# Moving the homes of the rounded weights by 256, 128 and 64 bytes, away from the remainder that their moving tiles have

## What is computed

```python
def mamba(x):                       # H=1024, DIN=2048, N=16, K=4, R=64
    x, z = split(x @ in_proj_w)     # input projection, 1024 -> 4096
    xc = silu(causal_conv(x) + conv_b)
    dt, Bm, Cm = rmsnorm of three slices of (xc @ x_proj_w.T)
    dt = softplus(dt @ dt_proj_w.T + dt_bias)
    y = selective_scan(xc, dt, -exp(A_log), Bm, Cm)
    return ((y + D * xc) * silu(z)) @ out_proj_w.T

def cross_attention(x, ctx):        # 16 heads of 96, 4 key/value heads, 1536 keys
    q, k, v = x @ Wq.T, [ctx, x] @ Wk.T, [ctx, x] @ Wv.T
    return softmax(q @ k.T / sqrt(96)) @ v @ Wo.T

def ffn(x):                         # 1024 -> 3584 -> 1024
    return (silu(x @ w1.T) * (x @ w3.T)) @ w2.T

x = layernorm(x + mamba(x))
x = layernorm(x + cross_attention(x, ctx))
x = layernorm(x + ffn(x))
```

## Time and profile before

| | |
|---|---|
| median of three runs | 3108.57 us |
| lowest and highest | 3108.5 and 3111.01 us |
| span of the profiled execution | 3110.0 us |
| granted TensorE clock, mean over the span | 0.965 of 2.4 GHz |
| TensorE matmul busy | 2874.5 us, 92% |
| VectorE busy | 2392.1 us, 77% |
| GpSimd busy | 1703.0 us, 55% |
| ScalarE busy | 1576.3 us, 51% |
| instructions | 35600, of them 11962 matmul records |

### The profile page before, as it was taken

One profiled execution on the slowest core, in us unless ns is written; L12 is line 12 of the kernel. 1 busy time (PEld: TensorE's weight loads), 2 busy tenths in 40 slices (PEclk: granted clock), 3 DMA queues, 4 the chain that ended last, 5 costly groups with the idle time before them and its releaser, 6 DMA issues. The chain is left out here.

```text
span 3110.0 us, 35600 instructions
## 1 busy us (share of the span) xinstructions
PE 2874.5 (92%) x11962; PEld 2040.6 (66%) x11962; DVE 2392.1 (77%) x2147; ACT 1576.3 (51%) x2679; POOL 1703.0 (55%) x952
## 2 busy tenths in 40 slices
PE   8996688888888988999999999989979999999998
PEld 7872344443222356887888888867758888887886
DVE  6568999999999957334777777765798888875667
ACT  4449555555665543214888888862332333334443
POOL 0004999999999933404887888851025444430034
PEclk9995799999989999999999999999989999999999
DMA  4228876766865662332111111215235555557554
GB/s 149 84 78 271 270 196 168 184 156 159 259 189 146 189 244 95 109 116 69 36 34 35 35 36 36 69 55 183 78 129 190 178 185 186 184 177 262 193 175 147
DMA packets 217400, 445.83 MB, mean 143 GB/s; under 512 B 33677, under 2 KB 47757, under 8 KB 215117
## 3 DMA queue, kind: packets, MB, share of 16 engines
q1 hardware_dynamic: 179502, 390.73, 40.5%
q10 hardware_dynamic: 37728, 52.96, 5.3%
HBM read 313.45 MB, written 130.15 MB: 143 GB/s over the span
## 5 line engine op out<-in xcount | busy, mean ns | idle before, releaser
L1834 POOL TENSOR_TENSOR at_p_lo<-at_p,at_p_hi 128x512 fp32r<-128x512 f32 x384 | 513.2, 1343 | 271.1 <-ACT at_p_hi L1746 257.7
L710 POOL TENSOR_TENSOR scan_dbx<-scan_u,scan_b_bc 128x1024 f32<-128x1024 f32 x256 | 596.6, 2367 | 0.0
L879 ACT ACTIVATE mamba_ps<-scan_dt,scan_a_neg 128x512 f32<-128x512 f32 (+1 forms) x512 | 332.0, 680 | 313.9 <-DVE scan_g L897 289.1
L908 DVE TENSOR_TENSOR_SCAN mamba_ps<-mamba_ps,scan_dbx 128x1024 f32<-128x1024 f32 x195 | 439.9, 2283 | 5.3 <-ACT mamba_ps L881 3.9
L1773 DVE TENSOR_REDUCE at_neg_max<-heads_ps 128x1 fp32r<-128x1536 f32 x128 | 225.0, 1758 | 144.9 <-PE heads_ps L1844 143.1
L102 PE MATMUL ff_ps<-ff_x_hi,ff_w_hi 128*128 128x512 f32 x784 | 309.4, 395 | 18.6 <-DVE ff_u L2449 6.4
L103 PE MATMUL ff_ps<-ff_x_lo,ff_w_hi 128*128 128x512 f32 x784 | 307.7, 392 | 0.0
L104 PE MATMUL ff_ps<-ff_x_hi,ff_w_lo 128*128 128x512 f32 x784 | 307.5, 392 | 0.0
L2673 POOL TENSOR_TENSOR ff_raw<-ff_raw,ff_scale 128x2048 f32<-128x2048 f32 x28 | 102.5, 3662 | 343.9 <-DMA ff_raw<-in_w 343.9
L1742 ACT ACTIVATE at_p<-heads_ps 128x512 f32<-128x512 f32 x384 | 228.3, 595 | 120.7 <-PE heads_ps L1868 98.4
L1746 ACT ACTIVATE at_p_hi<-at_p 128x512 fp32r<-128x512 f32 x384 | 242.8, 632 | 12.2
(11 more groups left out here) (295 smaller groups left out, 6953.0 us busy)
## 6 DMA issues: line engine op xcount, KB each, us to landing
scan_dt<-dt SPq DMA_DIRECT2D x120, 256.0 KB, 4.9
scan_u<-u SPq DMA_DIRECT2D x120, 256.0 KB, 7.9
ff_raw<-in_w SPq DMA_DIRECT2D x56, 512.0 KB, 4.8
ff_down_ar<-ac SPq DMA_DIRECT2D x98, 256.0 KB, 2.8
ff_down_hr<-hc SPq DMA_DIRECT2D x98, 256.0 KB, 2.7
ff_act_w<-in_w SPq DMA_DIRECT2D x14, 1024.0 KB, 7.3
hc<-ff_act_t SPq DMA_DIRECT2D x56, 256.0 KB, 6.1
ac<-ff_act_v SPq DMA_DIRECT2D x56, 256.0 KB, 5.8
```

The costliest lines, as they stand in the source:

```text
L710: nc.gpsimd.tensor_tensor(dbx[n % SL][:].rearrange("p (h l) -> p h l", h=2), u[it % 2][:, c:c + 2], b_bc[b][:, k // 2].unsqueeze(1).to_bro ...
L879: nc.scalar.activation(at[:, h * L + h:(h + 1) * L], dt[it % 2][:, c, h:L], ACT.Exp, scale=a_neg[:, it % IT, e:e + 1]).then_inc(a_ready, 1)
L908: nc.vector.tensor_tensor_scan(out[:], ps_a[n % SA], dbx[n % SL][:], 0.0, ALU.mult, ALU.add).then_inc(scanned, 1)
L1834: nc.gpsimd.tensor_tensor(p_lo[n % NSL][:], p[n % NSL][:], f32(p_hi[n % NSL][:]), ALU.subtract).then_inc(p_lo_done, 1)
```

## The change

It moves addresses and nothing else. In `mamba_in` the running address goes up by 256 bytes ahead of `w_hi` and by another 256 behind `w_lo`: the four rounded weight tiles get the remainder 0 while the moving tiles keep 256, and what follows them lies 512 bytes higher, with the remainder it had. In the last stage the address goes up by 64 ahead of `w_hi`: the weight buffers of the feed-forward part get the remainder 320 against 256 of the moving tiles. With them everything behind goes up by 64 (the partial sums `p0`, `u2`, `u3`, `u4`, the raw weights, the landing tiles `ar` and `hr`, the scales). The tiles for the output product of the heads start from that address too, and a second step of 64 behind `wo0` puts `wo_hi` and `wo_lo` 128 bytes above the old remainder, at 384. The instructions of each engine, their order, operands and waits are the same as before.

```diff
--- before.py
+++ after.py
@@ -214,8 +214,10 @@
     x_lo = Arena(nc, "in")("x_lo", [P, HT, TOK], F32R)
     dtw = Arena(nc, "in_dtw", sb.at)("dtw", [R + 1, IT, P])
     w = [sb(f"w{s}", [P, HT, P]) for s in range(2)]
+    sb.at += 256
     w_hi = [sb(f"w_hi{s}", [P, HT, P], F32R) for s in range(2)]
     w_lo = [sb(f"w_lo{s}", [P, HT, P], F32R) for s in range(2)]
+    sb.at += 256
     xz = [sb(f"xz{s}", [P, B, L + KC - 1]) for s in range(2)]
     acc = [sb(f"acc{s}", [P, B, L]) for s in range(2)]
     pre = [sb(f"pre{s}", [P, B, L]) for s in range(2)]
@@ -1993,6 +1995,7 @@
 
     a_raw = [ahead.a, Arena(nc, "ff_raw", sb.at)("a_raw", [P, KT, L])]
     w_hi, w_lo = [], []
+    sb.at += 64
     for s in range(NW):
         if s == NW - 1:
             wo_at = Arena(nc, "ff_wo", sb.at)
@@ -2001,6 +2004,7 @@
     p0, u3 = sb("p0", [P, L]), sb("u3", [P, L])
     u2, u4 = ([sb(f"{n}{s}", [P, L]) for s in range(2)] for n in ("u2", "u4"))
     wo[0] = wo_at("wo0", [P, KH, P])
+    wo_at.at += 64
     wo_hi, wo_lo = ([wo_at(f"wo_{part}{s}", [P, KH, P], F32R) for s in range(2)] for part in ("hi", "lo"))
     assert wo_at.at <= sb.at
     down_at = Arena(nc, "ff_down", sb.at)
```

## The result

The changed kernel takes 3130.48 us (median of 4 runs, 3129.11 to 3134.7), the kernel before 3108.53 beside it (4 runs, 3099.54 to 3111.01). The ratio is 1.0081, with a 95% interval of 1.0068 to 1.0094: slower by 22 us where 34 were forecast. The profiled execution has a span of 3129.9 us at a mean granted clock of 0.966.

The account below looks back on a forecast made before the run. TensorE's matmul pace was taken to bound the kernel; 6.5 + 3 + 22.6 + 2 is 34.1 us, which on the profiled 3110.0 us, less 1.4 for the median, gives 3143 us, with a range of 3098 to 3160.

Parts of the forecast that it names:

- What bounds the kernel: Whole span: TensorE is busy for 92% of it, so most of a change in its pace would reach the end.
- The pace depends on the homes: Steady matmul streams: 0.2266 us a matmul for equal remainders of weights and moving tile, 0.2342 for unequal ones.
- The displacement clears the collision: Rival, all three displaced parts: displacement separates weight and moving reads, so faster, 3061 us, or 3085 to 3102; chance 0.22.
- Homes don't matter: Rival, all three displaced parts: the query product is slow for another reason or these displacements are harmless; 3108.6 us, chance 0.14.
- One price for all three displacements: Input projection, output product, feed-forward part: +7.6 ns a matmul for 256, 128 and 64 bytes alike.
- a pace that differs between the three parts: Sign in the profile after: it would say the displacement's size counts, which the single price ignores; no size given.
- Input projection, 6.5 us: Input projection, displaced by 256 bytes: 850 matmuls x 7.6 ns, 6.5 us slower, all on the path.
- the case of 3136 us: Rival, input projection: 256 bytes as good as 0, its term goes, 3136 us; 0.64 includes forecast's 0.5 and half-cost 64 bytes.
- Output product, 3 us: Output product of the heads, 128 bytes: some 500 full-clock matmuls, 3.8 us, partly hidden in shrinking waits; 3 us taken.
- Feed-forward part, 22.6 and 2 us: Feed-forward part, 64 bytes: 2976 matmuls x 7.6 ns, 22.6 us, plus 2 us for its start and tail.
- Everything else at new homes: Raw weights, partial sums and landing tiles only shift; VectorE does not care about homes, so this costs nothing.
- A fast pace as a state that disturbances end: TensorE's streams: a run of equal steps falls into the fast pace, 0.227 us; a disturbance ends it for a while.

Follow-up runs that it names:

- experiment 1: Against the kernel before, only the feed-forward weights moved by 64 bytes, output product kept aligned: 3128.88 us against 3107.82, ratio 1.0071.
- experiment 6: Against the kernel before, feed-forward rounded weights moved by 64 bytes, tiles behind them by 256, back at their old remainders: 3129.49 us, ratio 1.0064.
- experiment 5: Against the kernel before, 96 bytes added ahead of `mid_h_hi`, so only the query product's homes are aligned: 3101.89 us against 3108.06, ratio 0.9981.
- experiment 7: Against the kernel before, distances of 32 bytes in input projection, 96 in output product, 192 in feed-forward part: 3123.14 us against 3108.06, one execution.
- experiment 2: Against the kernel before, only 256 bytes in the input projection and 128 in the output product of the heads: 3111.78 us, ratio 1.0012.
- experiment 12: Against the kernel before, input projection with 97 rows in the first pass, 96 in the second and third: 3114.18 us against 3111.28.

## Why the prediction was right, and where it was off

**What bounds the kernel: right.** TensorE's pace in its full stretches reached the end nearly whole. The feed-forward products grew by 21.1 us and the span by 19.9.

**The pace depends on the homes: right, and shown both ways.** Moving the weights away costs 21 us (experiments 1 and 6), moving the query product's moving tile to distance 0 gains 6 (experiment 5). "The displacement clears the collision" falls: no distance was faster than 0. "Homes don't matter" falls as well, and with it, for this kernel, the rule of the two independent read ports, which the Trainium skill states in SBUF — State Buffer, "Who interferes with whom", and under which it would have been certain.

**One price for all three displacements: the step that failed.** The prediction took +7.6 ns, measured in the query product, for 256, 128 and 64 bytes alike. It gave the distance there as 416 - 256 = 160; as weights less moving tile it is -160, or 96 modulo 256, the slowest distance of all. For that distance the price was exact (experiment 5 gets it back, experiment 7 shows it in another stage); 160 itself costs 6.6 ns (0.2333 us). The step from this one price to the other sizes failed. The prediction had named the sign of it, a pace that differs between the three parts, and it came: 0.2267, 0.2323 and 0.2333 us.

- *Input projection, 6.5 us.* It was 0. The prediction measured its remainders after 512, the length of a row of weights; here 256 bytes give the pace of 0, and in the output product of experiment 1 too. This was named among the rivals as the case of 3136 us, but not taken; the measured 3130.48 lies nearer to that case than to 3143.
- *Output product, 3 us.* 0.3 in the profiled execution after, 2.8 in experiment 2. Each step became some 6 ns longer in full-clock stretches (0.2323 to 0.2333 us for 0.2267), about 3 us over some 500 steps, and the stage's idle time took up part of it or not.
- *Feed-forward part, 22.6 and 2 us.* 64 bytes cost 0.2333 - 0.2266 = 6.7 ns, so 2976 x 6.7 is 19.9, not 22.6. With the tail it measured 21.1 in all. The two terms were 3.5 too high together.

The sum by measured terms is 0 + 0.3 to 2.8 + 21.1, 21.4 to 23.9 us, and the result 22 (by the medians) to 25 (the ratio of 1.0081 on 3108.5). The forecast of 34 is this plus 6.5 for the input projection, 3.5 for the feed-forward part and the rest for the output product.

**Everything else at new homes: right.** VectorE's tiles behind the weights cost nothing (experiment 6 against 1), and no new wait appeared.

**A fast pace as a state that disturbances end: borne out in part.** A pass of 97 rows among those of 96 ends it (experiment 12), 96 rows throughout, short sums or a busy GpSimd do not. What in the memory or the array makes 0.2267 and 0.2333 the two paces, and why even equal homes stay above the 0.216 of the earlier trace rows, no run here shows.

## What to carry to other kernels

When a stage runs with TensorE full, compare its start-to-start time with that of stages of the same shape: a few nanoseconds a matmul are worth tens of microseconds and don't show in busy shares or waits. For float32r products in three passes, give weights and moving tile homes that are equal modulo 256, which one line in an arena does. Passes of unequal rows are worth a trial without the odd row: one mix, 97 among 96, was seen to cost as much as unequal homes. And before one price is carried over to other sizes, look whether the trace holds the size that the change uses; if none does, each size is an unknown of its own.

## What the runs showed of the chip that was not expected

- The pace of a 128x512 float32r matmul at full clock depends on the distance of two homes modulo 256: 0.2267 us at 0, 0.2290 at 192, 0.2323 to 0.2344 at all other multiples of 32. It is the distance that counts and not either home, so the reads of the two tiles are not free of each other in this stream; what couples them no run shows.
- One pass of 97 rows between passes of 96 costs every pass 6 to 7 ns, at equal homes (0.2333 us for 0.2267); 96 rows alone cost nothing.
- GpSimd products over 480 columns, with both inputs in SBUF, stretched VectorE's 1024-column steps with two large inputs in SBUF from 1285 to 2098 ns, and left TensorE's pace as it was.
